# Interleaving state and variance products with expert products, a regrouped last stretch, and an earlier tanh on ScalarE

## Time and profile before

| | us |
|---|---|
| median of three runs (range) | 670.16 (669.15 to 670.27) |
| the profiled execution, own time | 668.51 |
| its span | 666.5 |
| TensorE matmul busy | 617.7 (93%) |
| VectorE busy | 513.2 (77%) |
| ScalarE busy | 438.9 (66%) |
| GpSimd busy | 360.7 (54%) |
| granted clock, mean | 0.997 |

### The profile page before, as it was taken

The page is one execution under the profiler, slowest core; times in us unless marked ns, Lnnn a source line. Parts: engine busy times, 40 slices in busy tenths (PEclk is TensorE's granted clock), DMA queues, the critical chain, the costliest instruction groups (busy, mean ns, idle before and its releaser), DMA issues.

```text
span 666.5 us, 18884 instructions
## 1 busy us (share of the span) xinstructions
PE 617.7 (93%) x5023; PEld 428.4 (64%) x5057; DVE 513.2 (77%) x1856; ACT 438.9 (66%) x1323; POOL 360.7 (54%) x441
## 2 busy tenths in 40 slices
PE   2484998789999999999999999999999999999998
PEld 0463775556677776766777767666766667676635
DVE  4998879677777877777777778787878787877664
ACT  6892774124777766676777676667777776666783
POOL 3002999233366656565555565555665555555563
PEclk9999999899999999999999999999999999999999
DMA  6200000102444444444444444444444444444354
GB/s 212 116 0 1 1 0 1 40 31 78 103 103 111 107 113 122 109 106 103 103 103 103 103 103 103 103 103 103 103 103 104 104 103 103 105 112 112 80 112 96
DMA packets 61622, 60.42 MB, mean 91 GB/s; under 512 B 22124, under 2 KB 57052, under 8 KB 61084
## 3 DMA queue, kind: packets, MB, share of 16 engines
q1 hardware_dynamic: 59164, 59.36, 36.9%
q10 hardware_dynamic: 2240, 0.73, 0.5%
q0 software_dynamic: 192, 0.01, 0.0%
HBM read 55.20 MB, written 4.89 MB: 90 GB/s over the span
## 4 chain that ended last, share of the span: by engine, by line
PE 81%; DVE 9%; ACT 5%; issue 3%; DMA 1%; SPq 0%; ACTq 0%; POOL 0%; DVEq 0%; POOLq 0%
PE bank L1577 15%; PE bank L1447 13%; PE bank L1565 8%; PE bank L1566 7%; PE bank L1508 5%; PE bank L1528 4%; PE bank L1469 4%; ACT skill_rows L683 3%; PE bank L1482 3%; PE bank L1353 2%; PE bank L1458 2%; PE bank L1306 2%; PE bank L1344 2%; PE bank L1486 2%; PE bank L1335 2%
## 5 line engine op out<-in xcount | busy, mean ns | idle before, releaser
L683 ACT ACTIVATE skill_rows<-bank,b1T,w_scale 128x512 f32<-128x512 f32 x256 | 196.6, 778 | 20.3 <-PE bank L1566 14.5
L516 POOL TENSOR_TENSOR feat_parts<-skill_rows 128x512 f32<-128x512 f32 x62 | 79.0, 1274 | 90.0 <-DVE feat_parts L1048 85.6
L1577 PE MATMUL bank<-skill_rows,w_sb 128*64 128x256 f32 x928 | 116.4, 382 | 0.0
L1447 PE MATMUL bank<-feat_parts 128*128 128x256 f32 (+1 forms) x512 | 102.2, 333 | 1.4 <-DVE feat_parts L1048 0.9
L1577 PEld LDWEIGHTS bank<-skill_rows,w_sb 128*64 128x64 f32 x928 | 63.1, 137 | 37.4 <-issue 11.0
L1447 PEld LDWEIGHTS bank<-feat_parts 128*128 128x128 f32 x512 | 79.7, 191 | 7.5 <-DVE feat_parts L1048 1.6
L1048 DVE TENSOR_TENSOR_SCAN feat_parts<-same,feat_parts 128x512 f32<-128x512 f32 x62 | 72.2, 1206 | 0.0
L1054 DVE TENSOR_TENSOR feat_parts<-bank,mask_sb 128x128 f32<-128x128 f32 x128 | 36.7, 286 | 38.9 <-PE bank L1447 37.7
L707 ACT ACTIVATE bank<-bank 128x64 f32<-128x64 f32 x128 | 26.7, 220 | 50.9 <-PE bank L1537 50.9
L1141 DVE SCALAR_TENSOR_TENSOR skill_rows<-bank,b2T,skill_rows 128x256 f32<-128x256 f32 x120 | 49.7, 475 | 3.8 <-PE bank L1577 2.5
L1070 DVE SCALAR_TENSOR_TENSOR feat_parts<-bank,feat_parts 128x256 f32<-128x256 f32 x128 | 45.0, 413 | 7.7 <-PE bank L1508 7.7
(11 more groups left out here) (279 smaller groups left out, 1482.8 us busy)
## 6 DMA issues: line engine op xcount, KB each, us to landing
skill_rows<-w_d SPq DMA_DIRECT2D x32, 512.0 KB, 6.1
same<-factor_d SPq DMA_DIRECT2D x31, 512.0 KB, 5.5
feat_parts<-w_d SPq DMA_DIRECT2D x30, 512.0 KB, 6.4
skill_rows<-skill_row_d SPq DMA_DIRECT2D x4, 1024.0 KB, 7.6
out<-o_sb SPq DMA_DIRECT2D x28, 128.0 KB, 5.1
feat_parts<-w_d SPq DMA_DIRECT2D x4, 256.0 KB, 4.8
w_sb<-in_L_ffn_W ACTq DMA_DIRECT2D x2, 256.0 KB
w_d<-wT SPq DMA_DIRECT2D x32, 16.0 KB, 1.4
```

The costliest lines, as they stand in the source:

```text
L516: pool.tensor_tensor(half[:, n, :], tm[:, 2 * n, :], tm[:, 2 * n + 1, :], ALU.add).then_inc(po_half, 1)
L683: act.activation(hid[:, e, :], banks[e % len(banks)][:, :], ACT.Gelu, bias=b1T[:, e:e + 1], scale=w1_scale[:, e:e + 1]).then_inc(ac_gelu, 1)
L1447: last = pe.matmul(n_bank[sc % 2][:, 0:SPAN[sc]], xs[:, k, sc * P:(sc + 1) * P], xs[:, k, sc * P:sc * P + SPAN[sc]], start=(k == 0), stop= ...
L1577: last = pe.matmul(z_bank[q % 2][n * D:(n + 1) * D, at:at + S // 2], w2_sb[:, e, :], hid[:, e, n * (S // 2):(n + 1) * (S // 2)], start=Tru ...
```

## The change

No product is added or dropped in the turns, their order changes. `state_of` and `attn_var` now issue one matmul per call. In the turn, each of the four state matmuls stands behind one f16 matmul of hidden 2 and 3, and each of the two variance matmuls behind one of hidden 5. `logits` moves ahead of hidden 1. On ScalarE `tanh` moves ahead of gelu 3 and of the squares. In the drain TensorE issues the hidden products of `b` in two blocks of four with one block of outputs behind them, and moves `weights_T(c)`, the folds and the outputs; ScalarE's `weights_T(c)` goes behind gelu 7 of `b`. The first four weighted products of the last sequence are added on VectorE (`last_pairs`, then `last_halves`), so that TensorE adds five blocks instead of eight.

```diff
@@ ScalarE turn
                 if att:
                     state_copy(i)
+                if rt:
+                    tanh(t)
                 if mlp:
                     gelu(k, 3)
                 if res:
                     h_square(r)
-                if rt:
-                    tanh(t)
@@ ScalarE drain
-                for e in range(4, 6):
+                for e in range(4, E):
                     gelu(b, e, drain_h)
                 weights_T(c)
-                for e in range(6, E):
-                    gelu(b, e, drain_h)
@@ VectorE
+            def last_pairs():
+                dve.wait_ge(dv_last, 4)
+                dve.tensor_tensor(last_two[:, 0], last_tm[:, 0], last_tm[:, 1], ALU.add).then_inc(dv_two, 1)
+            def last_halves():
+                dve.wait_ge(dv_two, 1)
+                dve.tensor_tensor(last_one[:, 0], last_two[:, 0, 0:S // 2], last_two[:, 0, S // 2:S], ALU.add)\
+                   .then_inc(dv_one, 1)
@@ VectorE drain
                 drain_weigh(a, 3)
+                drain_weigh(b, 0)
+                drain_weigh(b, 1)
                 drain_finish(B - 4)
-                for q in range(NP):
-                    drain_weigh(b, q)
+                drain_weigh(b, 2)
+                drain_weigh(b, 3)
                 drain_finish(a)
-                for q in range(NP - 1):
-                    drain_weigh(c, q)
+                drain_weigh(c, 0)
+                drain_weigh(c, 1)
+                last_pairs()
+                drain_weigh(c, 2)
+                last_halves()
+                drain_weigh(c, 3)
                 drain_finish(b)
-                drain_weigh(c, NP - 1)
                 last_finish()
@@ TensorE
-            def state_of(b):
+            def state_of(b, k, c):
 ...
+                last = pe.matmul(zB[:, k * D:(k + 1) * D], x_rows[:, c, k * P:(k + 1) * P], ub[:, c, :],
+                                 start=(c == 0), stop=(c == 1))
+                if k + c == 2:
+                    last.then_inc(pe_state, 1)
@@ TensorE drain
-                drain_hidden(b, 0)
                 centred_T(c)
-                drain_hidden(b, 1)
+                for e in range(4):
+                    drain_hidden(b, e)
                 logits(c, 1)
                 drain_out(a, 3)
-                drain_hidden(b, 2)
-                drain_hidden(b, 3)
+                for e in range(4, E):
+                    drain_hidden(b, e)
                 drain_out(b, 0)
-                drain_hidden(b, 4)
-                drain_hidden(b, 5)
                 drain_out(b, 1)
                 weights_T(c)
-                drain_hidden(b, 6)
-                drain_hidden(b, 7)
-                drain_fold(B - 4)
                 for e in range(4):
                     drain_hidden(c, e)
+                drain_fold(B - 4)
                 drain_out(b, 2)
-                drain_out(b, 3)
                 drain_hidden(c, 4)
                 drain_hidden(c, 5)
-                drain_out(c, 0)
+                drain_out(b, 3)
                 drain_fold(a)
                 drain_hidden(c, 6)
                 drain_hidden(c, 7)
-                drain_out(c, 1)
-                drain_out(c, 2)
+                for q in range(NP):
+                    drain_out(c, q)
+                drain_fold(b)
+                pe.wait_ge(ac_gelu, E * B)
                 for e in range(2):
-                    last_fold(0, e)
-                drain_fold(b)
-                drain_out(c, 3)
-                for q in range(1, NP):
-                    for e in range(2):
-                        last_fold(q, e)
+                    last_expert(2, e)
+                pe.wait_ge(dv_one, 1)
+                last_fold(last_one[:, 0])
+                for e in range(2):
+                    last_expert(3, e)
@@ TensorE turn
+                if rt:
+                    logits(t, side)
                 if mlp:
                     hidden(k, 1, 1 - side)
-                if rt:
-                    logits(t, side)
 ...
+                for n in range(NK):
+                    if mlp:
+                        hidden_high(k, 2 + n, 1 - side)
+                    if att:
+                        state_of(i, n, 0)
+                    if mlp:
+                        hidden_low(k, 2 + n, 1 - side)
+                    if att:
+                        state_of(i, n, 1)
                 if mlp:
-                    hidden(k, 2, 1 - side)
-                if att:
-                    state_of(i)
-                if mlp:
-                    hidden(k, 3, 1 - side)
                     expert_out(k, 0, i)
 ...
                 if mlp:
-                    hidden(k, 5, 1 - side)
+                    hidden_high(k, 5, 1 - side)
                 if att:
-                    attn_var(i)
+                    attn_var(i, 0)
+                if mlp:
+                    hidden_low(k, 5, 1 - side)
+                if att:
+                    attn_var(i, 1)
```

More of the change, by code:

```diff
@@ L199, in program @@
         last_tm = over(parts_flat, 2 * S, NP, S)
+        last_two, last_one = over(parts_flat, 9 * S + CAUSAL, 1, S), over(parts_flat, 10 * S + CAUSAL, 1, S // 2)
         idle_rows = pm[:, 0:16]
@@ L1460, in input_rows @@
                 last.then_inc(pe_rows, 1)
-            def state_of(b):
[L1464 to L1471, removed]
+            def state_of(b, k, c):
+                if k + c == 0:
+                    pe.wait_ge(po_ub, b + 1)
+                    pe.wait_ge(ac_rows, b + 1)
+                    wait(pe, dv_tm, NP * (b - 3) if not isinstance(b, int) or b >= 4 else 0)
+                last = pe.matmul(zB[:, k * D:(k + 1) * D], x_rows[:, c, k * P:(k + 1) * P], ub[:, c, :],
+                                 start=(c == 0), stop=(c == 1))
+                if k + c == 2:
+                    last.then_inc(pe_state, 1)
             def values(b):
@@ L1511, in y_core, with attn_var @@
                             last.then_inc(pe_y, 1)
[L1513 to L1521, removed]
+            def attn_var(b, n):
+                if n == 0:
+                    pe.wait_ge(ac_sq, b + 1)
+                    if isinstance(b, int) and b == 0:
+                        pe.wait_ge(ones_set, 4)
+                last = pe.matmul(az[:, C * D + 2 * n:C * D + 2 * n + 2], a_sq[:, n * P:(n + 1) * P], ones_d[:, n, :],
+                                 start=True, stop=True)
+                if n == 1:
+                    last.then_inc(pe_var, 1)
             def z_out(b):
@@ L1558, in logits, with hidden_high @@
                 last.then_inc(pe_lg, 1)
-            def hidden(b, e, side):
+            def hidden_high(b, e, side):
                 if isinstance(b, int) and b + e == 0:
@@ L1565, in hidden, with hidden_low @@
                 pe.matmul(h_bank[e % 2][:, :], w1k[:, 0, e, :], xT[side][:], start=True, stop=False)
+            def hidden_low(b, e, side):
                 pe.matmul(h_bank[e % 2][:, :], w1k[:, 1, e, :], xT[side][:], start=False, stop=True).then_inc(pe_hid, 1)
+            def hidden(b, e, side):
+                hidden_high(b, e, side)
+                hidden_low(b, e, side)
             def expert_out(b, q, turn_now=None):
@@ L1631, in drain_fold, with last_fold, last_expert @@
                 fold(b, 4)
-            def last_fold(q, e):
-                if q + e == 0:
-                    pe.wait_ge(ac_gelu, E * B - 2)
-                pe.wait_ge(dv_last, 2 * q + e + 1)
[L1638 to L1643, removed]
+            def last_fold(rows, first=False, last=False):
+                for c in range(2):
+                    done = pe.matmul(h_bank[c][:, 0:P], rows[:, c * P:(c + 1) * P], ident_f[:], start=first, stop=last)
+                if last:
+                    done.then_inc(pe_fold, 1)
+            def last_expert(q, e):
+                pe.wait_ge(dv_last, 2 * q + e + 1)
+                last_fold(last_tm[:, q, e * (S // 2):(e + 1) * (S // 2)], first=(2 * q + e == 4), last=(2 * q + e == E - 1))
             def drain():
```

1 line of the change is left out of this document (added).

## The result

The changed kernel takes 661.16 us (median of three runs, 660.15 to 662.61) against 670.16: ratio 0.9861 [0.982, 0.9903]. The forecast was 663.7, with a range of 659.0 to 667.5. Its profiled execution took 661.16, span 659.0.

A forecast was written before the change was run, and what follows sets the result against it. TensorE was taken to bound the kernel, with ScalarE level at gelu 4. Turns 5.8 plus drain 0.7 gave 6.5 us off: 662.0 from the profiled 668.51, 663.7 from the median 670.16; range 659.0 to 667.5.

The forecast's parts named there:

- TensorE's savings: Turns: interleaving state matmuls with f16 ones saves 0.18 us, variance about 0.09, earlier logits 0.09; hidden 6 ready 0.36 earlier.
- The variance's 0.09: Turns, TensorE: interleaving the two variance matmuls hides one more weight load, saving about 0.09 us ahead of hidden 6.
- ScalarE's order: Turns: later state copy, then tanh; gelu 3 and squares stay, gelu 4 starts 0.18 to 0.20 us earlier.
- None of them was ahead of TensorE: Turns: VectorE's late second expert output and gates didn't delay TensorE, so ending its tanh wait is worth nothing by itself.
- 0.20 a turn: Turns: net saving per turn after ScalarE's limit on gelu 4; times 29 turns, 5.8 us.
- the drain, 0.7: Drain: fewer TensorE passes and the new order end the kernel 0.7 us earlier; bounds -0.3 and 2.4.
- the end is tied to the last sequence's weights: Drain: the weights' DMA sets the end, as VectorE idled 0.72 us for a DMA at 659.61.
- the store is free of the fetch: Drain rival: the last weights' store misses the instruction fetch, gaining 1.7 us more, 662.0 us; chance 0.10.
- Nothing hides: Turns rival: interleaving hides no more weight loads; 0.02 us a turn plus the drain's 0.7, 668.9 us; chance 0.10.
- the weave costs: Turns rival: six more f16/float32 changes cost 0.09 us each, 0.34 a turn slower, 679.4 us; chance 0.07.
- ScalarE doesn't bind: Turns rival: all 0.36 us a turn arrives, 10.4 in total, plus the drain's 0.7, 659.1 us; chance 0.08.
- The last stretch doesn't hold: Drain rival: pairs and halves delay the late products, losing the 0.7 us, 664.4 us; inside the forecast, no separate chance.

The follow-up runs named there:

- e1: Changed kernel with the state and variance matmuls back in blocks instead of interleaved with f16 matmuls; 666.2 us, 0.9945 of the kernel before.
- e5: Changed kernel with the four logit matmuls back behind hidden 1; 664.1 us, 0.991 of the kernel before.
- e2: Changed kernel with only the two variance matmuls back together behind hidden 5; 662.07 us, 0.9871 of the kernel before.
- e6: Kernel before with only the tanh moved ahead of gelu 3 in the turns; 670.32 us, 1.0001 of the kernel before.
- e3: Changed kernel with the tanh back behind the squares, in the turns only; 662.86 us, 0.9891 of the kernel before.
- e4: Changed kernel's turns with the old drain order on ScalarE, VectorE and TensorE; 664.33 us, 0.9896 of the kernel before.
- e10: Changed kernel with an extra small load, waited for, ahead of loading the last weights; 661.93 us, 0.9859 of the kernel before.
- e9: Changed kernel without VectorE's two adds in the drain, TensorE adding all eight blocks; 663.54 us, 0.9867 of the kernel before.
- e8: Changed kernel with hidden 4 ahead of y_core, gelu 4 ahead of x_p, next turn's input products behind hidden 6; 664.23 us, 0.9903 of before.

## Why the prediction was right, and where its sizes were off

*TensorE's savings: right.* The pair is 0.38 from f16 to f16, the block 1.63, logits 0.090, all within 0.02 of the sum's terms (e1, e5). The variance's 0.09 is lost in the wait, as forecast (e2).

*ScalarE's order: right.* State copy, tanh, gelu 3 and squares stand within 0.03 of where they were put. That the tanh costs nothing at its new place and earns nothing alone: shown by e6. That it earns nothing within the whole change: wrong by 0.054 a turn, 1.6 us (e3). "None of them was ahead of TensorE" held for the old TensorE; the woven one reaches the next update earlier, and there the gates had become late.

*Mis-sized: 0.20 a turn, measured 0.256.* The term was "GpSimd's norm doesn't move, `x_p<-xc` starts at 320.54". It starts 0.07 earlier in the turn, 9.22 instead of 9.29, with a norm that begins at the same place. The overlap was wrong: VectorE's two short instructions no longer fall on GpSimd's power, which is 0.065 shorter for it (e6). `x_p<-xc` waits for the norm, gelu 4 starts right behind it, and TensorE waits for gelu 4. So gelu 4 starts 0.25 earlier, hidden 6 too, and the wait is 0.09, not 0.15. No run changed the power alone: e3 has the long power too, but there the squares start 0.11 earlier and make up for it, and its 0.054 is the gates' wait. Over 29 turns 0.256 is 7.4 instead of 5.8.

Over the 28 distances 6.75 was measured, where 7.2 would be due: two turns of that execution, between 195 and 227 us, took 0.15 and 0.28 longer, at a granted clock of 1.00. In both ScalarE began gelu 3 late, and TensorE waited for gelu 4. In the first, gelu 3 started 0.25 behind the tanh instead of 0.10; all ten kernels with the early tanh show it in that turn, and its cause is open. In the second, a VectorE instruction took 1.30 instead of 0.19 (the last section). TensorE's row:

```profile
225.81 0.39 PE L1582 MATMUL bank<-xT_odd,w1k 128*128 128x512 f16 x1 [0.20 <-ACT skill_rows L685]
```

*Mis-sized: the drain, 0.7, measured 1.87. Here a step failed:* "the end is tied to the last sequence's weights". VectorE's 0.72 of idle time for a DMA at 659.61 was real, but TensorE came free of its expert products only at 660.6 and went on into its 24 passes without a hole; the chain of waits of that stretch shows TensorE from 645 to 663. The end was TensorE's count of instructions and their order: the sums are worth 0.78, the order 1.08. That 1.87 lies within the bounds given for the drain is luck, for the upper one, 2.4, stood on the store's 1.7. The store did go from 3.1 to 1.4:

```profile
w_d<-wT SPq DMA_DIRECT2D x1, 16.0 KB, 1.4
```

so the condition of the rival "the store is free of the fetch" came true, and its price, 1.7, was nil in the old drain (e4, e6). In the new one the early store is needed: e10. In the new drain TensorE no longer owns the end alone: between 650.3 and 653.5 the chain that ended last is VectorE's products of the last sequence.

*The sum.* Turns 7.2 less 0.4, tail 2.1, token stage 1.3 the other way: 7.5 of span. Medians differ by 9.0, because the profiled execution of before was a quick one, as the forecast said. The forecast, 663.7, was 2.5 too high: 1.2 of it in the drain and 1.2 in the turns (6.75 and the tail's 0.23, less 5.8), the rest of the token stage's noise.

*The rivals.* "Nothing hides" and "the weave costs" fall with 0.38 from f16 to f16. "ScalarE doesn't bind" falls with e2: 0.09 a turn still disappears before hidden 6. "The last stretch doesn't hold" falls with e9: without the sums the end comes 0.78 later.

## What to carry to other kernels

Price a reordering on a full engine by distances from start to start, and follow each saving to the next place where another engine is level: 0.09 us ahead of the state was worth 0.09, and 0.09 behind it nothing. An idle row that names a DMA does not say that the DMA sets the end: look at what the engine that ends last was doing at that time, and at its chain. When one engine gets quicker, "was never late" has to be worked out anew for everything that feeds it.

## What the runs showed of the hardware

- An instruction of GpSimd may depend on its neighbours: the power on 128x4 takes 1.006 to 1.021 us, and 1.072 to 1.083 where VectorE's `pick<-pick,wgt` and `w_flat<-pick` run beside it (all 384 of the 12 traces).
- VectorE's `lg<-lg,br_sb` takes 0.19 us, but twice in the changed kernel 1.04 and 1.30, beside a GpSimd instruction of 1.27 us (rows of both engines in the long turn, then in the drain, then VectorE's line: least, median and most ns):

```profile
217.96 1.27 POOL L522 TENSOR_TENSOR feat_parts<-feat_parts 128x512 f32<-128x512 f32 x1
217.98 1.30 DVE L1095 TENSOR_TENSOR lg<-lg,br_sb 128x32 f32<-128x32 f32 x1
```

```profile
638.10 1.27 POOL L518 TENSOR_TENSOR feat_parts<-skill_rows 128x512 f32<-128x512 f32 x1
...
638.38 1.04 DVE L1095 TENSOR_TENSOR lg<-lg,br_sb 128x32 f32<-128x32 f32 x1
```

```profile
L1095 DVE TENSOR_TENSOR lg<-lg,br_sb x32: 191/192/1302, 156.5 to 638.4; 128x32 f32<-128x32 f32 x32
```

  Both long ones end 0.05 behind GpSimd's instruction (639.42 and 639.37 in the drain, where the tanh of the last sequence waited 0.64 for it). In every turn the two instructions start within 0.05 us of each other, and a few nanoseconds decide. In the 12 traces all 19 long ones (1.04 to 1.31 us) start 6 ns or more behind GpSimd's. In the turns, where VectorE is ahead or less than 6 ns behind, it takes 0.19 (at 6 ns there is one of each). The Trainium skill, "SBUF — State Buffer", section "Who interferes with whom", says that a VectorE instruction with two inputs in SBUF contends with a GpSimd instruction that reads SBUF, and calls the ports that they share an exclusive lock; the trace agrees.
- The tile's shape costs at its change: 0.10 us from 512-column f16 matmuls to a 64-row tile (e8), as to 64-column tiles in the earlier trace rows.
- A 16 KB instruction fetch can hold up a 16 KB store. In the kernel before, the fetch began 1.08 us behind the store's issue and held its DMA engine 0.92, and the store took 3.1 us. In e8 it began 0.59 ahead and held the engine 1.23, and the store took 1.74. In the ten others it began 1.5 us or more ahead, and the store took 1.4. What places the fetch isn't shown: in e6 TensorE's code is that of before, and the fetch had moved too. With one trace of each kernel, chance isn't ruled out.
